# Both biases of an expert out of a table made in DRAM at the start, and the early tile list built in three pieces

## The reference

```python
def step(y, params):
    W1e, b1e, W2e, b2e, ge = params
    h = jax.nn.gelu(jnp.einsum('bld,df->blf', x, W1e) + b1e, approximate=False)
    out = jnp.einsum('blf,fd->bld', h, W2e) + b2e
    return (y + ge[..., None] * out, None)
```

## Time and profile before

| | us |
|---|---|
| median of three runs (lowest, highest) | 791.67 (788.38, 793.95) |
| the profiled execution's own time | 789.1 |
| its span in the trace | 787.4 |
| PE busy | 696.4 (88%) |
| DVE busy | 458.7 (58%) |
| ACT busy | 373.0 (47%) |
| POOL busy | 390.6 (50%) |
| mean granted TensorE clock | 0.956 |

### The profile page before, as it was taken

One profiled execution on the slowest core, in us unless ns is written; L12 is line 12 of the kernel. 1 busy time (PEld: TensorE's weight loads), 2 busy tenths in 40 slices (PEclk: granted clock), 3 DMA queues, 4 the chain that ended last, 5 costly groups with the idle time before them and its releaser, 6 DMA issues.

```text
span 787.4 us, 22691 instructions
## 1 busy us (share of the span) xinstructions
PE 696.4 (88%) x7841; PEld 598.7 (76%) x7841; DVE 458.7 (58%) x1331; ACT 373.0 (47%) x891; POOL 390.6 (50%) x599
## 2 busy tenths in 40 slices
PE   0695689999999999999698999999999999999970
PEld 0583456777777777776467999899999999999970
DVE  7301356788888888888855664344444444444448
ACT  0122256666666666666354433334443354334353
POOL 6771123567777777777455553333344334433320
PEclk9996599999999999999889999999999999999995
DMA  7725544444444444444229543758338425399159
GB/s 206 136 41 150 146 112 103 102 103 117 109 109 108 113 112 113 110 110 112 49 74 260 153 122 88 215 142 236 106 102 232 110 88 149 111 285 247 50 179 327
DMA packets 92667, 108.98 MB, mean 138 GB/s; under 512 B 16545, under 2 KB 81058, under 8 KB 92258
## 3 DMA queue, kind: packets, MB, share of 16 engines
q1 hardware_dynamic: 80786, 80.64, 39.8%
q0 software_dynamic: 11792, 27.18, 11.4%
HBM read 140.32 MB, written 32.34 MB: 219 GB/s over the span
## 4 chain that ended last, share of the span: by engine, by line
PE 62%; DVE 12%; issue 9%; POOL 8%; DMA 3%; SPq 3%; ACT 2%; POOLq 1%; DVEq 0%; ACTq 0%
PE BK L483 20%; PE BK L495 20%; PE BK L821 4%; PE BK L947 3%; PE BK L906 2%; PE BK L958 2%; DVE negmax L1527 2%; POOL slot_rows L1856 2%; POOL rs L1805 2%; PE BK L926 2%; DMA level_patches<-pixels 1%; DVE hr L686 1%; PE BK L873 1%; POOL hr L1845 1%; PE BK L469 1%
## 5 line engine op out<-in xcount | busy, mean ns | idle before, releaser
L514 ACT ACTIVATE pixels<-BK,b1t 128x128 f32<-128x128 f32 x474 | 131.1, 375 | 203.1 <-PE BK L483 203.1
L483 PE MATMUL BK<-pixels,shared 64*128 64x128 f32 x2844 | 175.5, 274 | 2.1 <-issue 2.1
L495 PE MATMUL BK<-shared,pixels 64*128 64x192 f32 x1896 | 174.0, 328 | 1.9 <-DVE pixels L662 1.6
L483 PEld LDWEIGHTS BK<-pixels,shared 64*128 64x128 f32 x2844 | 172.3, 189 | 2.7 <-issue 2.7
L696 POOL DMA_INDIRECT pair_rows<-pixels x79 | 78.0, 987 | 189.9 <-DVE pixels L662 185.0
L495 PEld LDWEIGHTS BK<-shared,pixels 64*128 64x128 f32 x1896 | 154.8, 187 | 3.9 <-issue 3.7
L1527 DVE TENSOR_REDUCE negmax<-BK 128x6 f32<-128x1536 f32 x64 | 112.4, 1757 | 24.7 <-PE BK L926 23.4
L1288 ACT ACTIVATE shared<-BK 128x1536 f32<-128x1536 f32 x64 | 92.7, 1449 | 9.8 <-PE BK L947 9.1
L1856 POOL DMA_INDIRECT slot_rows<-xr,adr x64 | 64.8, 1013 | 36.6 <-issue 13.7
L661 DVE TENSOR_TENSOR pixels<-BK,shared 128x192 f32<-128x192 f32 x79 | 28.2, 358 | 70.9 <-PE BK L495 70.6
L648 DVE TENSOR_TENSOR pixels<-pixels 128x1 int32<-128x1 f32 x64 | 10.2, 160 | 90.6 <-PE BK L469 90.6
(11 more groups left out here) (241 smaller groups left out, 1075.6 us busy)
## 6 DMA issues: line engine op xcount, KB each, us to landing
shared<-ew SPq DMA_DIRECT2D x158, 288.0 KB
shared<-ew SPq DMA_DIRECT2D x79, 576.0 KB
shared<-qk_parts SPq DMA_DIRECT2D x112, 96.0 KB
shared<-eb SPq DMA_DIRECT2D x79, 96.0 KB
pixels<-slot_rows POOLq DMA_DIRECT2D x64, 104.0 KB
qk_parts<-shared SPq DMA_DIRECT2D x32, 192.0 KB, 2.0
shared<-qk_parts SPq DMA_DIRECT2D x16, 288.0 KB
shared<-pair_rows SPq DMA_DIRECT2D x12, 384.0 KB, 7.7
```

The source lines that it names most:

```text
L483: last = nc.tensor.matmul(hidden(t)[h * HC + c], w1h[w][rows, (k + h) % NK, c * P:(c + 1) * P], xtT[p][rows, k, :], start=(c == 0 and k == ...
L495: last = nc.tensor.matmul(Y[h], hT[p][rows, c * P:(c + 1) * P], w2b[w][rows, c, :], start=(c == 0), stop=(c == FC - 1))
L514: last = nc.scalar.activation(hT[p][:, c * P:(c + 1) * P], hidden(t)[c], ACT.Gelu, bias=b1t[:, c, t:t + 1])
```

## The change

A DRAM tensor `bias_d` of 16 x 128 x (6 + 192) fp32 is written at the very start by seven DMAs that ACT issues: one that copies b2 of each expert to 128 rows, and six that put b1 in the columns ahead of it, so that row p of expert e holds b1[e, c*128 + p] for c = 0 to 5 and then all of b2[e]. SP loads a [128, 198] block of it for each new expert, ahead of w2b. The products with the one-hot matrix, b1r, b1t, b2b and the copies go. `early_table` is split into `early_ends`, `early_entries` and `early_lists`, put at three places in step 14 of DVE, and `early_taken`, put ahead of `table_ends` after the images. The running sum over 16 experts is made in padded buffers.

```diff
+    bias_d = nc.dram_tensor("expert_biases", (NE, P, FC + E), fp32).ap()
...
         def moe_loads(sp):
             sp.wait_ge(s["r_early"], 2)
             sp.wait_ge(s["pe_st"], U * LAST)
+            sp.wait_ge(s["st_bias"], 16 * FC + 16)
...
             def second(t, e, new):
                 w = t % NW
+                wait_prev(sp, s["m_y"], t - NW + 1)
+                sp.dma_start(bias[w][:, :], bias_d[ds(e, 1), :, :].rearrange("a p n -> p (a n)"), cond=new) \
+                    .then_inc(s[f"m_b{w}"], 16)
                 wait_prev(sp, s["m_s2"], t - NW + 1)
                 sp.dma_start(w2b[w][:, :, :], ew2[ds(e, 1), :, :].rearrange("a (c p) d -> p (a c) d", p=P),
-                             cond=new) \
-                    .then_inc(s[f"m_wb{w}"], 16)
-                wait_prev(sp, s["m_y"], t - NW + 1)
-                sp.dma_start(b2b[w][:, :], eb2[ds(e, 1), :].rearrange("a d -> (a d)").partition_broadcast(P),
                              cond=new) \
                     .then_inc(s[f"m_wb{w}"], 16)
...
-        def early_b1(pe):
-            pe.wait_ge(s["ld_b1"], 16)
-            pe.wait_ge(s["r_early"], 3)
-            for c in range(FC):
-                last = nc.tensor.matmul(M0[:, c * NEARLY:(c + 1) * NEARLY], b1r[:, c * P:(c + 1) * P], b1e[:, 0:NEARLY],
-                                        start=True, stop=True)
-            last.then_inc(s["pe_b1"], 1)
...
             if t == NEARLY:
-                pe.wait_ge(s["dve_b1"], 2)
+                pe.wait_ge(s["r_tab"], 1)
...
         def t_gelu(act, t):
             p = t % 2
-            if t == 0:
-                act.wait_ge(s["dve_b1"], 1)
+            w = t % NW
+            act.wait_ge(s[f"m_b{w}"], 16 * (t // NW) + 16)
             act.wait_ge(s["m_s1"], t + 1)
             wait_prev(act, s["m_s2"], t - 1)
             for c in range(FC):
-                last = nc.scalar.activation(hT[p][:, c * P:(c + 1) * P], hidden(t)[c], ACT.Gelu, bias=b1t[:, c, t:t + 1])
+                last = nc.scalar.activation(hT[p][:, c * P:(c + 1) * P], hidden(t)[c], ACT.Gelu, bias=bias[w][:, c:c + 1])
             last.then_inc(s["m_gelu"], 1)
...
-        def running(dve, te):
+        def running(dve, first, a, b):
             V = nc.vector
-            c, d, sh = 0, 1, 1
-            while sh < NE:
-                V.tensor_copy(te[d][:, 0:sh], te[c][:, 0:sh])
-                then(dve, V.tensor_tensor(te[d][:, sh:NE], te[c][:, sh:NE], te[c][:, 0:NE - sh], ALU.add))
-                c, d, sh = d, c, 2 * sh
-            return te[c]
+            c, sh = first, 1
+            for d in (a, b, a, b):
+                then(dve, V.tensor_tensor(d[:, PAD:], c[:, PAD:], c[:, PAD - sh:PAD + NE - sh], ALU.add))
+                c, sh = d, 2 * sh
+            assert sh == NE == 2 * PAD
...
-        def early_table(dve):
+        every = run_f[1][:, PAD:].unsqueeze(1).to_broadcast([P, NEARLY, NE])
+
+        def early_ends(dve):
             V = nc.vector
             dve.wait_ge(s["r_early"], 1)
-            then(dve, V.tensor_copy(r_ci[:, :], seen_c[:, :]))
-            then(dve, V.tensor_scalar(r_ti[:, :], r_ci[:, :], P.bit_length() - 1, None, ALU.arith_shift_right))
-            V.tensor_copy(seen_f[:, :], r_ti[:, :])
-            then(dve, V.tensor_copy(r_te[0][:, :], r_ti[:, :]))
-            ends = running(dve, r_te)
-            every = ends[:, :].unsqueeze(1).to_broadcast([P, NEARLY, NE])
-            V.tensor_tensor(seen_g[:, :], seen_f[:, :], ends[:, :], ALU.subtract)
+            then(dve, V.tensor_scalar(seen_i[:, PAD:], seen_i[:, PAD:], P.bit_length() - 1, None, ALU.arith_shift_right))
+            running(dve, seen_i, *run_f)
+
+        def early_entries(dve):
+
+            V = nc.vector
+            V.tensor_scalar(seen_g[:, :], seen_i[:, PAD:], float(-P), float(SEG), ALU.mult, ALU.add)
             then(dve, V.tensor_tensor(seen_le[:, :, :], every, early_place[:, :].unsqueeze(2).to_broadcast([P, NEARLY, NE]),
                                       ALU.is_le))
-            V.tensor_scalar(seen_g[:, :], seen_g[:, :], float(NEARLY), 0.0, ALU.add, ALU.max)
-            V.tensor_reduce(r_tfs[:, 0:NEARLY], seen_le[:, :, :], AX.X, ALU.add)
-            then(dve, V.tensor_tensor(seen_st[:, :, :], seen_le[:, :, :], every, ALU.mult))
-            V.tensor_tensor(taken[:, 0:NE], seen_g[:, :], seen_f[:, :], ALU.min)
-            then(dve, V.tensor_reduce(seen_s[:, :], seen_st[:, :, :], AX.X, ALU.max))
-            V.tensor_copy(tab[:, 0:NEARLY], r_tfs[:, 0:NEARLY])
-            then(dve, V.tensor_tensor(seen_x[:, :], early_place[:, :], seen_s[:, :], ALU.subtract))
+            V.tensor_tensor(seen_st[:, :, :], seen_le[:, :, :], seen_g[:, :].unsqueeze(1).to_broadcast([P, NEARLY, NE]),
+                            ALU.mult)
+            then(dve, V.tensor_reduce(r_tfs[:, 0:NEARLY], seen_le[:, :, :], AX.X, ALU.add))
+
+        def early_lists(dve):
+
+            V = nc.vector
+            then(dve, V.tensor_reduce(seen_s[:, :], seen_st[:, :, :], AX.X, ALU.add))
             V.tensor_tensor(r_new[:, NW:NEARLY], r_tfs[:, NW:NEARLY], r_tfs[:, 0:NEARLY - NW], ALU.not_equal)
-            then(dve, V.tensor_scalar(seen_r[:, :], seen_x[:, :], float(P), float(P), ALU.mult, ALU.add))
-            V.scalar_tensor_tensor(rowi[:, 0:NEARLY], r_tfs[:, 0:NEARLY], float(SEG), seen_r[:, :], ALU.mult, ALU.add) \
-                .then_inc(s["r_early"], 1)
-            V.tensor_scalar(b1e[:, 0:NEARLY], r_tfs[0:NE, 0:NEARLY], pid[0:NE, 0:1], None, ALU.is_equal) \
-                .then_inc(s["r_early"], 1)
-
-        def early_bias(dve):
-            dve.wait_ge(s["pe_b1"], 1)
-            nc.vector.tensor_copy(b1t[:, :, 0:NEARLY], M0[:, 0:FC * NEARLY].rearrange("p (c t) -> p c t", t=NEARLY)) \
-                .then_inc(s["dve_b1"], 1)
+            V.tensor_scalar(tab[:, 0:NEARLY], r_tfs[:, 0:NEARLY], 0.0, None, ALU.add)
+            V.tensor_tensor(rowi[:, 0:NEARLY], early_base[:, :], seen_s[:, :], ALU.add).then_inc(s["r_early"], 1)
+
+        def early_taken(dve):
+
+            V = nc.vector
+            then(dve, V.tensor_tensor(seen_g[:, :], seen_i[:, PAD:], run_f[1][:, PAD:], ALU.subtract))
+            then(dve, V.tensor_scalar(seen_g[:, :], seen_g[:, :], float(NEARLY), 0.0, ALU.add, ALU.max))
+            then(dve, V.tensor_tensor(taken[:, 0:NE], seen_g[:, :], seen_i[:, PAD:], ALU.min))
...
-            then(dve, V.tensor_tensor(ysum[r][:, :], Y[0], b2b[w][:, :], ALU.add))
+            then(dve, V.tensor_tensor(ysum[r][:, :], Y[0], bias[w][:, FC:FC + E], ALU.add))
...
-            sp.dma_start(b1r[:, :], eb1).then_inc(s["ld_b1"], 16)
...
-                    if isinstance(i, int) and i == SEEN + 3:
-                        early_b1(pe)
                     b_lg(i - 2)
...
-                pe.wait_ge(s["dve_pr"], j + 1)
-                late_b1(pe)
                 t_down(pe, 10)
...
+            nc.scalar.dma_start(bias_d[:, :, FC:FC + E], eb2.unsqueeze(1).to_broadcast([NE, P, E])).then_inc(s["st_bias"], 16)
+            for c in range(FC):
+                nc.scalar.dma_start(bias_d[:, :, c:c + 1], eb1[:, c * P:(c + 1) * P].unsqueeze(2),
+                                    allow_slow_non_contiguous=True).then_inc(s["st_bias"], 16)
             act.wait_ge(s["ld_const"], n_const)
...
                     f_hst(i + 2)
+                if isinstance(i, int) and i == SEEN + 3:
+                    early_ends(dve)
                 if on(0):
                     a_max(i, 3)
                 if on(2):
...
                     b_yn(i - 2)
                 if on(-3):
                     b_top(i - 3)
+                if isinstance(i, int) and i == SEEN + 3:
+                    early_entries(dve)
                 if on(-1):
                     b_on(i - 1, 0)
                 if on(-3):
                     b_count(i - 3, q)
+                if isinstance(i, int) and i == SEEN + 3:
+                    early_lists(dve)
                 if on(-1):
                     b_on(i - 1, 1)
                 if on(2):
                     f_qk(i + 2, 0, s["act_q"], s["dve_q"])
-                if isinstance(i, int) and i == SEEN + 3:
-                    early_table(dve)
...
+                early_taken(dve)
                 table_ends(dve)
```

More of the change, by code:

```diff
@@ L230, in vit_tower @@
         x2c = sb("x2c", [P, TT, E])
-        b1r = sb("b1r", [NE, FF])
-        b1t = sb("b1t", [P, FC, NTILE])
         place_i = sb("place_i", [P, NEARLY], i32)
         early_place = sb("early_place", [P, NEARLY])
+        early_base = sb("early_base", [P, NEARLY])
+        PAD = NE // 2
+        seen_i = sb("seen_i", [P, PAD + NE], i32)
+        run_f = [sb(f"run_f{k}", [P, PAD + NE]) for k in range(2)]
+        run_t = [sb(f"run_t{k}", [P, PAD + NE]) for k in range(3)]
         taken = sb("taken", [P, NE + 1])
@@ L257, in vit_tower @@
         r_ti = late([P, NE], i32)
-        r_te = [late([P, NE]) for k in range(2)]
         r_le = late([P, NE])
@@ L273, in vit_tower @@
         r_new = late([P, NTILE], i32)
```

(27 more changed lines are left out.)

15 lines of the change are left out of this document (3 added, 12 removed).

## The result

The changed kernel took 800.61 us (median of 8 runs, 795.1 to 807.07), the kernel before 792.09 us beside it: ratio 1.0095, 95% interval 1.0062 to 1.0128. One of the eight, 807.07, was a slow execution and is left out of the ratio. A second measurement on a like chip gave 805.14 (4 runs) against 792.67, ratio 1.0184 (1.0135 to 1.0233). The forecast was 788.6 us; rival 1, the start that pays for the whole table, had 799.9. The profiled execution after took 802.69 us, its span 801.0.

What follows compares the result with a forecast made beforehand. PE bounds most of the run (62% of the chain), transfers matter in the start; -3.75 - 1.2 - 2.9 + 0.3 + 0 - 0.5 + 5.0 = -3.05 gives 788.6 us, own range 785.7 to 798.0, over all 780 to 803.

Steps and rivals of the forecast that it cites:

- rival 1: Start pays for the whole table, ACT and SP sharing q1: +16.3 us in place of +5.0, 799.9 us; chance 0.24.
- F: Start: b1r's load goes, -0.5 us; seven table DMAs delay the start's own packets, +5.0 us (ends 3.4 and 12.9).
- A: Step 14, DVE: the early list leaves the path PE waits on, 0.8 of 4.56 us staying: -3.75 us.
- B: After step 14's wait: PE's 6.40 us at granted clock 0.58 may not come; -1.2 us (ends 0 and -2.7).
- C: Two sets of b1 products on PE's chain go, -1.44 and -1.48 us: -2.9 us in all.
- rival 2: Start hides the table and both low-clock stretches go, the one in 404 to 411 giving 1.8: 780.3 us; chance 0.25.
- D: Drain: early_taken on the path of the tables, less copies saved by the padded running sum: +0.3 us (0 to +0.6).
- E: Expert stage, load order: biases ahead of W2, W2 about 1 us later, hidden by 3 to 5 us of lead: 0.
- the prediction's own sign: Expert stage: a stall of ACT ahead of a gelu, or PE ahead of a down, from a DMA would show E wrong.
- the load of b1r: Start: one SP issue in the first 13 us, ahead of the pixels' way to DRAM, goes: -0.5 us.

Runs made afterwards that it cites:

- e4: Kernel before with the seven table DMAs added at ACT's start, nobody reading the table: 814.57 against 792.67 us; ratio 1.0275, on the second kind of chip 1.0131.
- e6: e5 with the three list pieces together at the old place ahead of a_max(15, 0): 821.74 against 814.77 us, then 818.12 against 815.78, second kind of chip.
- e1: Changed kernel with the seven table DMAs moved behind the start, issued by SP: 788.72 against 792.67 us for the kernel before; second kind of chip 813.25 against 822.55.
- e5: Changed kernel with b1 transposed once on PE, table written by two DMAs behind the start: ratio 0.9892, 0.9923, 0.9904 to the kernel before, second kind of chip.
- after_again: Second profile of the changed kernel, nothing altered, on a chip like the first: 805.14 us against 792.67 for the kernel before, ratio 1.0184.

## Why the prediction was wrong

**The step that failed is F, the seven DMAs at the start**: +5.0 forecast, 20.7 and 21.9 us by the offsets at maximum 5 of the two pairs, 21.9 by adding the seven DMAs alone (e4). Four things in it:

- *The wide packets.* The sum took 34 ns, the price of 768 bytes out of SBUF, and 4.4 us of every engine. DRAM to DRAM they took 78 ns in the mean, 10 us of recorded time in every engine. The first of them took 46 ns and the later ones 107, so no one price holds for them. Whether the two ends, the source that is one row of b2 read 128 times, or the crowd of packets makes them dear was not tested.
- *The single numbers.* 9.3 ns, not 13: this term was too dear, and the range 8.7 to 33.5 held it. The rule of the Trainium skill ("DMA: Bandwidth & Descriptors", "Specifications"), that a transfer under 512 bytes is read, modified and written, makes them no dearer here than other tiny runs; the 28.0 ns that the prediction took for it is three times too much.
- *How delay arises.* The sum let each own packet wait for one foreign packet, and nothing else: 386 x 13 ns. The runs show three other ways, all at nothing in the sum. The index list is late, and the gathers with it (8.36 and not 3.47). SP's own issues take longer, so that the last constant goes out at 19.73 and 29.27 in the two profiles of the changed kernel (12.27 before). ACT is held in issuing, which alone keeps PE's fold until 49.95 (33.24 before). The first two and the longer transfers make one chain, and which of the two leads it changes from profile to profile.
- *What is not F.* The 4.5 us by which the clock makes the first pair worse between maximum 1 and 5 are in the second profile of the kernel before too. The delay that the table makes is the one at maximum 1: 16.2 us in the first pair, 21.7 in the second.

By the measured prices the table is 768 x 9.3 ns + 10 us = 17.1 us in every engine. Rival 1's form, "the table's time less what was idle", makes of it 17.1 - 3.5 = 13.6 us, an estimate from rows of these traces: nearer than +5.0, and still 3 to 8 us short. Its first reason (one queue row for ACT and SP) is not so, since ACT has q10. Its reason that ACT is held is shown, but the transfers end later.

**A and B, the list off the path**: -4.95 forecast, -4.4 and -4.7 measured between maximum 59 and 64. That the sum came out is luck, for both terms were off and the errors cancel. A, from 59 to 61, is -1.9 in both pairs and not -3.75: the first piece costs 1.3 us that the idle time of DVE did not cover, and the way from 60 to 61 gives 3.2. By e6, which has the new list at the old place, some 1.5 of the 1.9 us are the shorter list (14.4 against 15.9) and only about 0.4 its place. B, from 61 to 64, is -2.5 and -2.8 and not -1.2, but not for the reason given: the low clock did not stay away, it came earlier (0.57 from 398 to 406), and in three of the profiles with the pieces it lasted 13 us and took the gain back.

**C, the products**: -2.9 forecast. The step from tile 11 to 12 went from 5.75 to 4.13 us, so the second set gave 1.6. From maximum 64 to t_up(0) 3.4 us go in the first pair and 1.25 in the second; the second is near the 1.44 of the first set of products. The first has more because the kernel before had its second low stretch of the clock (0.53) in that one profile; rival 2 priced it at 1.8 us, but it is not the change's doing.

**D** can't be told apart in these numbers. **E**, 0 forecast: W2 is late nowhere by it, but by the prediction's own sign (a stall of ACT ahead of a gelu, put down to a DMA) it was wrong: biases are late six times. The way from t_up(0) to the last products is 344.3, 346.3 and 346.1 us in three profiles with the old loads, 345.1, 341.7 and 343.5 in three with the new ones, all on the first kind; 1.6 of the mean difference of 2.1 is C. So E stays near 0 in time, within stalls of up to 7 us that fall on other tiles in each profile.

Without F the sum of the forecast was -8.05 with the load of b1r; the milestones give -7.1 in the first pair (20.7 less 13.6) and -10.4 in the second (21.9 less 11.4, rounded), and e4 beside the changed kernel 9.4. The total of the rest was right, parts of it by luck; one term of seven decided the sign. Of the range of the forecast alone, 785.7 to 798.0, the lower end does not follow from its parts: 788.6 - 1.6 - 1.5 - 0.3 is 785.2.

## What to carry to other kernels

Work that is "only DMA, early on" is not free where the start is a chain of small transfers: it delays each link, the issuing engines too, and moved to a later place it can delay what is being gathered there (e1). A row with the same length of run is no price yet for a transfer between other ends or in a crowd: bound it, and ask which link of the chain is hurt first and what the issues of many small runs do to the other issuing engine. Take a second profile of the kernel before ahead of putting a difference of the clock down to a change: here it undid two such readings. And a table whose layout needs single numbers can often be had by one transpose and fewer, longer runs: 2048 of 24 bytes for 12,288 single numbers in e5, whose two DMAs took SP 0.45 and 2.04 us to issue.

## What the runs showed of the hardware

- 12,288 single numbers in six DMAs held the issuing engine for 37.4 us (2.5 to 10.2 us for each DMA), while SP's own issues went from 0.43 to 1.27 us and more (up to 4.35 in after_again).
- 4 bytes from DRAM to DRAM took 9.3 ns of an engine. 768 bytes took 46 ns at first and 107 ns from 4 to 7 us, 78 in the mean.
- The stretch of granted clock 0.50 in the first images ended at about 100 us in one profile of the kernel before and at about 111 in the next, which made 4.3 us from maximum 1 to 5.
- Two kinds of chips differ by 30 us in the kernel before and by 24.5 in e1; in e1 PE's first block stands 27.7 us later on the second kind, behind one standing time of ACT and DVE.
